# Macaron block on one core: 128-wide output products as four column tiles of 32 tokens, the division in three tasks, column scales in silu, and new task orders

## The reference

```
x = x + 0.5 * ffn(layernorm(x))
x = x + attn(layernorm(x))
x = x + 0.5 * ffn(layernorm(x))

ffn(x):  h = layernorm(x) * ln_gamma + ln_beta
         y = silu(h @ w1 + b1)                       # 128 -> 512
         return x + 0.5 * (y @ w2 + b2)              # 512 -> 128
         # w = (int - 128) * scale of its column, both layers
attn(x): q, k, v of 16 heads of 8; s = relu(q k^T / sqrt(8))
         o = (s / (sum of s + 1e-6)) v
         return layernorm(x + o @ w_out + b_out) * gamma + beta
```

## Time and profile before

| | |
|---|---|
| median of 3 runs | 405.4 us (404.82 to 406.85) |
| the profiled execution | 403.35 us, span in the trace 401.6 us |
| PE busy | 388.8 us (97%) |
| DVE, ACT, POOL busy | 293.3, 219.4, 220.4 us |
| L429 (values) on PE | 137.3 us, 1024 passes |
| L414 (scores) on PE | 84.5 us, 512 passes |
| L397 (fc2), both stages, on PE | 66.2 us, 512 passes |

### The profile page before, as it was taken

One profiled execution on the slowest core, in us unless ns is written; L12 is line 12 of the kernel. 1 busy time (PEld: TensorE's weight loads), 2 busy tenths in 40 slices (PEclk: granted clock), 3 DMA queues, 4 the chain that ended last, 5 costly groups with the idle time before them and its releaser, 6 DMA issues.

```text
span 401.6 us, 7947 instructions
## 1 busy us (share of the span) xinstructions
PE 388.8 (97%) x2694; PEld 204.3 (51%) x2694; DVE 293.3 (73%) x682; ACT 219.4 (55%) x406; POOL 220.4 (55%) x446
## 2 busy tenths in 40 slices
PE   7979999999999999999999999999999999989986
PEld 6865534453454545553454445553464445323685
DVE  3365577978698868878698868877696868866760
ACT  2225466556747476457737476557737476536302
POOL 4548136655872759355972759354963655271052
PEclk9899999999999999999999999999999999989999
DMA  6216203500243005400252005400250004300001
GB/s 160 51 24 161 53 2 73 144 21 2 50 112 77 28 4 119 116 2 26 48 132 61 26 8 122 110 2 26 58 141 16 26 14 101 98 29 1 2 12 43
DMA packets 15977, 23.08 MB, mean 57 GB/s; under 512 B 4032, under 2 KB 5312, under 8 KB 15936
## 3 DMA queue, kind: packets, MB, share of 16 engines
q1 hardware_dynamic: 12528, 17.97, 18.3%
q10 hardware_dynamic: 3408, 4.59, 3.9%
HBM read 3.67 MB, written 2.10 MB: 14 GB/s over the span
## 4 chain that ended last, share of the span: by engine, by line
PE 76%; DVE 13%; issue 5%; ACT 2%; POOL 2%; DMA 1%; ACTq 0%; DVEq 0%; POOLq 0%
PE o_bank L429 27%; PE scores L414 14%; PE pre_bank L397 8%; PE post_bank L397 7%; DVE probs L808 5%; PE pre_bank L372 3%; PE post_bank L372 2%; PE pre_bank L373 2%; PE post_bank L468 2%; PE pre_bank L388 2%; PE pre_bank L367 1%; PE post_bank L373 1%; PE post_bank L388 1%; PE post_bank L367 1%; DVE den L697 1%
## 5 line engine op out<-in xcount | busy, mean ns | idle before, releaser
L808 DVE TENSOR_SCALAR probs<-scores 128x512 f32<-128x512 f32 x256 | 163.6, 680 | 45.4 <-PE scores L414 44.9
L600 ACT ACTIVATE probs<-scores 128x512 f32<-128x512 f32 x256 | 139.5, 597 | 101.0 <-PE scores L414 101.0
L429 PE MATMUL o_bank<-probs,v_op 128*32 128x512 f32 x1024 | 137.3, 608 | 0.0
L414 PE MATMUL scores<-q_op,k_op 32*128 32x512 f32 x512 | 84.5, 496 | 2.9 <-DVE probs L808 1.3
L414 PEld LDWEIGHTS scores<-q_op,k_op 32*128 32x128 f32 x512 | 34.7, 182 | 83.8 <-issue 48.3
L429 PEld LDWEIGHTS o_bank<-probs,v_op 128*32 128x32 f32 x1024 | 20.2, 108 | 31.7 <-issue 24.3
L837 POOL TENSOR_SCALAR norm_y_var<-norm_y_mv 128x4 f32<-128x4 f32 x8 | 1.7, 217 | 61.4 <-DVE norm_y_mv L673 61.4
L397 PEld LDWEIGHTS post_bank<-w,post_y 128*128 128x128 f32 x256 | 30.3, 191 | 9.1 <-issue 8.2
L397 PEld LDWEIGHTS pre_bank<-w,pre_y 128*128 128x128 f32 x256 | 29.9, 192 | 7.8 <-issue 7.6
L397 PE MATMUL post_bank<-w,post_y 128*128 128x128 f32 x256 | 33.5, 281 | 0.0
L397 PE MATMUL pre_bank<-w,pre_y 128*128 128x128 f32 x256 | 32.7, 281 | 0.0
(11 more groups left out here) (133 smaller groups left out, 543.3 us busy)
## 6 DMA issues: line engine op xcount, KB each, us to landing
q_op<-q_parts SPq DMA_DIRECT2D x64, 128.0 KB, 2.6
k_op<-k_parts SPq DMA_DIRECT2D x126, 64.0 KB, 2.1
pre_x<-in_L_attn_x_dram ACTq DMA_DIRECT2D x8, 256.0 KB, 2.7
out_dram<-o_rows ACTq DMA_DIRECT2D x8, 256.0 KB, 2.0
w_int<-in_L_ffn_fc_q_dram SPq DMA_DIRECT2D x2, 256.0 KB, 4.6
s_rows<-in_L_ffn_fc_scales_dram SPq DMA_DIRECT2D x2, 256.0 KB, 6.0
w_raw<-in_L_attn_w_qkv_dram SPq DMA_DIRECT2D x1, 192.0 KB, 8.3
wo<-in_L_attn_w_out_dram SPq DMA_DIRECT2D x8, 8.0 KB, 6.6
```

What stands on the lines that cost most here:

```text
L414: mm(scores[i][:, j, :], k_op[rows, g, P * kt:P * (kt + 1)], q_op[rows, g, :], start=True, stop=True).then_inc(scores_done[i], 1)
L429: last = mm(o_bank[pair][VW * j:VW * (j + 1), :], v_op[:, kt, heads_of(g).start + 2 * j, :], probs[:, s % 2, j, :], start=(odd == 0 and kt ...
L600: activation(probs[:, s % 2, j, :], scores[0][:, j, :], ACT.Relu).then_inc(probs_done[0], 1)
L808: v.tensor_scalar(probs[:, s % 2, 2 + j, :], scores[1][:, j, :], 0.0, None, ALU.max).then_inc(probs_done[1], 1)
```

## The change

- `by_tokens` takes the place of the products of fc2, v and op: for each 128 tokens four products with 32 tokens as weights, each into its own 32 partitions of the bank, with the same 128 columns moving. The mode of the array is then that of the values products. There are four times as many instructions.
- `oT` is cut into the tasks `oT`, `den` and `a`, which stand apart in the tables of DVE.
- The scale of a column of `w1` is no longer multiplied into `w1`, but is the scale of the silu (L532) and of the bias sum. The weights take one DVE instruction less and a transfer of 2 KB in place of 256 KB.
- k comes before q. Both parts of k go in one transfer: four transfers for a group of heads, six before.
- Where `fc1` is alone, its first two products no longer wait for `t_lo`.
- All tables are written anew, with other numbers of warm-up products.

```diff
+            def by_tokens(into, tokens, t, w, start, stop):
+                for j in range(HG):
+                    part = slice(P * t + VW * j, P * t + VW * (j + 1))
+                    last = mm(into[VW * j:VW * (j + 1), P * t:P * (t + 1)], tokens[:, part], w, start=start, stop=stop)
+                return last
...
                     for t in range(TT):
-                        last = mm(st.bank[:, P * t:P * (t + 1)], st.y[:, f, P * t:P * (t + 1)], w2[:, f, :],
-                                  start=f == 0 and t == 0, stop=f == FT - 1 and t == TT - 1)
+                        last = by_tokens(st.bank, st.y[:, f, :], t, w2[:, f, :], f == 0 and t == 0, f == FT - 1 and t == TT - 1)
...
+                    if alone(st, b):
+                        pe.wait_ge(st.t_hi_in, b + 1)
...
-                    next_fill(st, b, what)
+                    if not alone(st, b):
+                        next_fill(st, b, what)
                     two_products(into, w1_hi[:, cols], w1_lo[:, cols], st.t_hi[:, :])
+                    if alone(st, b):
+                        next_fill(st, b, what)
...
-                    activation(st.y[:, f, :], bank(st, b, what), ACT.Silu, bias=b1_sum[:, f:f + 1]
-                               ).then_inc(st.free, 1)
+                    activation(st.y[:, f, :], bank(st, b, what), ACT.Silu, bias=b1_sum[:, f:f + 1],
+                               scale=s1_col[:, f:f + 1]                               ).then_inc(st.free, 1)
...
-                dve.wait_ge(loaded, 32)
-                v.tensor_copy(w, w_int).then_inc(link, 1)
-                dve.wait_ge(link, 1)
-                return v.scalar_tensor_tensor(w, w, -ZERO_POINT, scales, ALU.add, ALU.mult)
...
+                dve.wait_ge(w1_loaded, 16)
+                v.tensor_scalar(w1[:, :], w1_int[:, :], -ZERO_POINT, None, ALU.add).then_inc(w_link, 1)
...
-                        if what == "k" and b == 0:
-
-                            act.wait_ge(high_in[1], 1)
-                            for c in range(2):
-                                act.dma_start(rows_to(k_op, 0, c, SLOTS), rows_of(qk_parts[1], 0, 0)).then_inc(qk_in[0], 16)
+                        if what == "q" and b == 0:
+
+                            act.wait_ge(high_in[0], 1)
+                            act.dma_start(rows_to(q_op, 0, 0), rows_of(0, 0, 0).unsqueeze(1).to_broadcast([ROW, 2, S])
+                                          ).then_inc(qk_in[0], 16)
...
 DVE_ORDER = [
-    ["oT.1@-1"],
-    ["aT@-1", "post.out@-2"],
+    ["oT.1@-1", "den.1@-1"],
+    ["a.1@-1", "post.out@-2", "aT@-1"],
```

More of the change, by code:

```diff
@@ L76 @@
     [],
-    ["post.store@-2"],
+    [],
     ["post.hT@-1"],
-    ["post.fc1.0@-1"],
-    ["pre.uT@1"],
-    ["post.fc1.1@-1", "pre.q@1"],
-    ["post.fc1.2@-1", "pre.k@1"],
-    ["post.fc1.3@-1", "pre.v@1"],
-    ["pre.hT@2"],
+    [],
+    ["pre.uT@1", "post.fc1.0@-1"],
+    ["pre.k@1", "post.fc1.1@-1"],
+    ["pre.q@1", "post.fc1.2@-1"],
+    ["pre.v@1"],
+    ["pre.hT@2", "post.fc1.3@-1"],
 ]
@@ L100 @@
     ["pre.x_stats@2"],
-    ["post.x2@-1", "post.x2_stats@-1"],
-    ["pre.x1@1"],
+    ["post.x2@-1"],
+    ["post.x2_stats@-1", "pre.x1@1"],
+    [],
     ["pre.x1_stats@1"],
@@ L106 @@
     [],
-    [],
+    ["oT.0", "den.0", "pre.k_lo@1"],
     ["pre.q_lo@1"],
-    ["pre.k_lo@1"],
-    ["oT.0"],
+    ["a.0"],
     ["pre.hT@2"],
@@ L292, in build, with rows_to, rows_of @@
         block = ctx.enter_context(nc.Block())
-        def rows_to(op, g, first, step):
-            return op[first::step, g, :].bitcast(F32)
-        def rows_of(parts, i, g):
-            return parts[ROW * g:ROW * (g + 1), i, :].bitcast(F32)
+        def rows_to(op, g, first):
+            return op[first::2, g, :].bitcast(F32)
+        def rows_of(i, parts, g):
+            return qk_parts[i][ROW * g:ROW * (g + 1), parts, :].bitcast(F32)
         @block.sync
@@ L336, in iteration @@
                             continue
[L337 to L342 removed]
+                        if g == 0:
+                            sp.wait_ge(pre.free, per * n + pre.n("q"))
+                        sp.dma_start(rows_to(q_op, g, i), rows_of(0, i, g).unsqueeze(1).to_broadcast([ROW, 2, S])
+                                     ).then_inc(qk_in[g], 16)
             for b in range(-1, B - 1):
@@ L451, in task @@
                         for t in range(TT):
-                            last = mm(bank(pre, b, "v")[:, P * t:P * (t + 1)], t_u[:, P * t:P * (t + 1)], wv[:, :],
-                                      start=True, stop=True)
+                            last = by_tokens(bank(pre, b, "v"), t_u, t, wv[:, :], True, True)
                         last.then_inc(pre.full, 1)
@@ L467, in task @@
                         for t in range(TT):
-                            last = mm(bank(post, b, "op")[:, P * t:P * (t + 1)], aT[:, P * t:P * (t + 1)], wo[:, :],
-                                      start=True, stop=True)
+                            last = by_tokens(bank(post, b, "op"), aT, t, wo[:, :], True, True)
                         last.then_inc(op_done, 1)
```

143 lines of the change are left out of this document (70 added, 73 removed).

## The result

| | before | after |
|---|---|---|
| median | 405.21 us (404.82 to 406.85, 4 runs) | 387.45 us (385.65 to 389.17, 4 runs) |
| the profiled execution, its span | 403.35 us, 401.6 us | 389.17 us, 387.4 us |
| first scores | 32.97 | 30.98 |
| first to last scores | 340.73 | 328.27 |
| after the last scores begin | 27.86 | 28.12 |

The ratio is 0.9554, with a 95% interval of 0.9503 to 0.9605. The change is faster, by 17.8 us in the medians and by 14.2 us between the two profiled executions. The forecast was 10.7 between the profiled executions and 394.7 for the median. The direction was right and the size too small. The 387.45 lies under the range of 389 to 403.

What follows compares the result with a forecast made beforehand. PE was taken as the bound, with some waits for DVE. Batches 8.3, start 1.5 and end 0.9 gave 10.7 off 403.35, so 392.7, or 394.7 as a median; range 389 to 403.

Steps and rivals of the forecast that it cites:

- Instructions: In the tiled blocks, four times the instructions bound PE: rounds of 0.135 to 0.16, about even to 424 us; chance 0.10.
- shown loads: In the tiled blocks, every round shows its loads: 0.133 a round, +2.0 a batch, time 402; chance 0.13.
- Passes and entries: PE's fc2, op and v as column tiles: 0.4 a batch from cheaper passes, 0.6 from entries and exits.
- The borders: Entering and leaving product forms on PE: 2.5 a batch becomes 1.9, free beside values, 0.14 for tiles standing apart.
- Waits: PE's waits at scores, in step 0 and steps 8 to 10: 2.28 a batch becomes 1.9, gain 0.4.
- the wait of step 0: PE's 1.19 wait at step 0's scores, behind DVE's division, should go because the division is split.
- the light end: Steps 5 to 10, with little other PE work: waits for DVE grow, 1.9 in all.
- the walk through DVE after `post_x`: Steps 5 to 8: `post_x` 2.9 after step 5's scores, relu of step 7 at 7.05, step 8's scores 1.5 late.
- The sum: A middle batch gains 0.4 passes, 0.6 entries and exits, 0.4 waits: 1.4, of which 1.2 was taken.
- The batches: Six batches gain 7.2 together, the last 0.8, the first 0.3: 8.3 in all.
- Start: Before the first scores: fc1 1.0 earlier, 0.5 from fewer transfers and warm-up passes; 1.5 in all.
- End: After the last scores: 0.65 from last fc1 products not waiting, 0.3 from eight blocks standing alone; 0.9 in all.

Runs made afterwards that it cites:

- the later one: A later profiled execution of the changed kernel, nothing changed, from a repeat timed beside another version on one chip: median 388.4 us, ratio 0.9567.

## Why the prediction was right in direction and too small

**Instructions, shown loads (first and second rival): no.** A round is 0.110 and a block 0.88. The forecast had 0.107, 0.133 for one rival and 0.16 and more for the other.

**Passes and entries: right mechanism, a little less.** The forecast was 0.4 + 0.6 = 1.0 a batch. Measured is 0.88, the 2.05 less the 1.17 of waits. 0.74 of it lies between the changed kernel and the one without tiles. The other 0.15 came with the new order alone (45.01 to 43.69, less 1.17 of waits), which has 13 stretches of 128-wide work where there were 14. The term for the passes was too large: ten blocks at 0.88 in place of 0.90 give 0.2, not 0.4. The borders gave the rest, nearly 0.7 for 0.6: where a block stands beside values, the pair takes 1.87 in place of 2.09, and with 64 columns 0.78 a batch is lost again. The price of a block that stands apart was in the forecast and shows as well. A wide block next to products of fc1, which have the full form too, is free (0.91 in the kernel without tiles); as tiles it takes 0.99 to 1.01.

**Waits: this step failed.** The forecast had 2.28 becoming 1.9, a gain of 0.4; they became 1.11, a gain of 1.17. That the wait of step 0 goes was right. That the light end grows from 1.09 to 1.9 was wrong; it stayed at 1.11. The step was the walk through DVE after `post_x`, with "nothing in that chain gets shorter, so I have it at 2.9". The same change had moved the silu of `fc1.3` from step 4 to step 3 on ACT, so that `y_apply` began 0.54 earlier and `post_x` at 2.31. Put back by experiment to 2.80, the waits are 1.57. The rest up to 1.9 is the walk's use of listed durations (0.90, 1.3, 1.25, 0.69), where start to start is 0.82, 1.20, 1.18 and 0.61: from `post_x` to the relu of step 7 it had 4.15, and there are 3.81. With both, the relu of step 7 has no delay, and step 8 waits only for the turn of 0.55 that it had before. And that the wait of step 0 went was not the cut alone, as forecast: with the division whole again 0.44 of its 1.19 came back.

**From the sum to 1.2.** The sum was 1.4, and 0.2 were taken off as a margin, which made the miss larger. With the waits as measured it would have been 2.2, near the measured 2.05.

**The batches.** Six batches were to gain 1.2 each, 7.2; they gained 2.92, four times 2.05 and 1.68: 12.8. The second batch gained most: its steps 0 to 2, which have no fc2 of an earlier batch beside them, took 9.07 and take 8.49, while those of a middle batch, with one more block and one more fc1 product in them, went from 11.04 to 11.61. The last batch gained 1.3 where 0.8 was forecast, with a low stretch in it on both sides. Batch 0 lost 1.7 where it was to gain 0.3; this is the low stretch, since the same kernel without it takes 36.49, as before (36.49).

**Start: 2.0 for 1.5, in part by luck.** fc1 began 1.36 earlier, where 1.0 was forecast. From fc1 to x1 another 1.53 were gained, 1.41 of it because fc1 ran at full clock, which the forecast had left open. 0.79 were lost again ahead of `u`, where the statistics waited for a load. The 0.5 for fewer transfers and warm-up products ahead of the first scores did not come: from `u` to the first scores are 9.66, and it was 9.55. No low stretch stands in fc1 in any profiled execution with the new start. In the profiled one of the changed kernel there is one in batch 0 instead, and there batch 0 gives back nearly all that the start gains; in the later one there is none, but its first scores come only at 32.22. In the ten profiled executions with this start and these loads (the kernel sorted by tile left out) the first scores lie between 30.09 and 32.22, so one pair of executions fixes this term to no better than a microsecond or two.

**End: -0.3 for 0.9.** The products of the last fc1 did save 0.4, 0.65 was forecast. But the new tables have four blocks behind the last values, where three stood before, and `op` stands behind all four though `aT` was ready 0.7 before `op` began (0.1 in the kernel before): 7.06 from the last scores to `op`, and it was 6.42. This wait stands in the new table for the end, and the forecast had looked only at the passes. The last fc2 takes 3.70, before 3.73 in its trace: no gain either.

**From the profile to the median.** The forecast added 2.05, which the profiled execution of before lay under its median. That of after lies 1.7 above its median. Its two low stretches are most of that: its mean granted clock is 0.991, and the other three executions have 0.995 to 1.00, which is one such stretch or none. Each costs 1.5 to 1.7 (last batch 35.19 with it and 33.64 without, batch 0 38.19 and 36.49). Of the 7.25 us that the forecast was too high, 3.75 come from this and 3.5 from the sum (10.7 for 14.2). Executions of one kernel differ here by as much as 4 us, and the profiled one stands anywhere among them.

## What to carry to other kernels

A small product pays for its form at its borders: give it the tiles of its neighbour in the queue, put passes for different tiles next to each other, and it enters free, even at four times the instructions (0.88 a block here, 0.90 as one tile). When a walk says that a chain keeps its length, look in the new order for what left each engine ahead of the chain, and walk with distances from start to start, not with listed durations. Where two engines hand a bank to and fro, count the shortest turn first: waits below it can't be won by giving one engine less to do.

## What the runs showed of the hardware that was not expected

- A low stretch of 3.4 us at a granted clock of 0.50 in batch 0 made that batch 1.7 to 1.8 longer (38.19 against 36.49 and 36.39). Another in the last batch cost 1.55. Together on one chip, the executions of the changed kernel took 387.06 at a mean clock of 1.00, 387.54 at 0.996, 388.2 to 388.72 at 0.991 and 390.89 at 0.986. Most of the spread of this kernel goes with the mean clock, that is, with how many low stretches there are; what brings one was not found.
- Four passes for four different tiles go in 0.110, so 32 in 0.88; sorted by tile, the same 32 need 2.37. Passes for a free tile started at 205.82, ahead of passes for another tile that stand before them in the program and started at 205.93.
- Silu with a column as its scale takes 0.78, with the scale left out 0.69. It hid here.
- `den` took 0.19, 0.56 and 0.95, and `a_t` 0.42 to 1.54, the same instruction each time. Where they began inside one of POOL's additions of 128x512 or its work on `v_op`, the rows above have them end 0.04 and 0.28 to 0.29 after it. In one place of the changed kernel both began within 0.02 (106.08 and 106.06): there `a_t` took 0.42 and POOL's addition 1.57 in place of 1.28. Beside POOL's 1.02 long `norm_x_rs` of 128x4 `den` took 0.19 (197.78). This is read from rows and not isolated.
- 512 bytes behind 64 KB in one queue landed 4.1 us later than ahead of them (8.4 and 4.3 after their issue, one profiled execution each). In two executions of the same kernel, the load of fc2's bias rows landed 2.2 apart.
